# An attention row in another order on TensorE: output product inside the projection, x turned behind the queries and keys, the values' product ahead of the transposes of E

## What is computed

```
h = shift_token(x); q, k, v = split(h @ wqkv, 3)           # 8 heads of 64
q, k = rotary(l2norm(q) * q_scale), rotary(l2norm(k) * k_scale)
sim  = (8 q) k^T, a token sees itself and the tokens before it (the window is all 128)
o    = softmax(sim) @ v
x    = x + o @ wo
```

## Time and profile before

| what | value |
|---|---|
| median of 3 runs | 2650.95 us (2649.64 to 2651.02) |
| profiled execution | 2650.9 us, span 2649.1 us |
| PE busy | 2582.9 us (98%), 25088 matmuls |
| DVE busy | 1916.7 us (72%) |
| ACT busy | 1702.0 us (64%) |
| POOL busy | 1422.8 us (54%) |
| chain that ended last | PE 89%, DVE 4%, issue 3%, ACT 2% |

### The profile page before, as it was taken

One profiled execution on the slowest core, in us unless ns is written; L12 is line 12 of the kernel. 1 busy time (PEld: TensorE's weight loads), 2 busy tenths in 40 slices (PEclk: granted clock), 3 DMA queues, 4 the chain that ended last, 5 costly groups with the idle time before them and its releaser, 6 DMA issues.

```text
span 2649.1 us, 71437 instructions
## 1 busy us (share of the span) xinstructions
PE 2582.9 (98%) x25088; PEld 2221.2 (84%) x25088; DVE 1916.7 (72%) x3779; ACT 1702.0 (64%) x4184; POOL 1422.8 (54%) x1512
## 2 busy tenths in 40 slices
PE   7999999979999999999999999999999999999998
PEld 5888888868888888887888887888888887888887
DVE  7777777668778887786655556788877878666664
ACT  4666666658777777774444446787877777444442
POOL 7888888567777776662100006777777665000000
PEclk9999999989999999999999999999999999999999
DMA  2111111111111111112111111111111111222221
GB/s 47 39 47 37 45 37 37 42 44 39 52 39 50 39 38 42 56 39 79 50 60 56 53 34 49 38 52 39 50 41 36 42 59 34 80 80 73 77 72 48
DMA packets 167250, 130.39 MB, mean 49 GB/s; under 512 B 24870, under 2 KB 165320, under 8 KB 167093
## 3 DMA queue, kind: packets, MB, share of 16 engines
q1 hardware_dynamic: 164789, 119.81, 14.8%
q0 software_dynamic: 2304, 8.47, 1.1%
HBM read 77.47 MB, written 50.33 MB: 48 GB/s over the span
## 4 chain that ended last, share of the span: by engine, by line
PE 89%; DVE 4%; issue 3%; ACT 2%; POOL 1%; DMA 1%; SPq 0%; POOLq 0%; DVEq 0%; ACTq 0%
PE const_banks L1409 6%; PE const_banks L1411 6%; PE const_banks L1410 6%; PE const_banks L1401 6%; PE const_banks L1402 6%; PE const_banks L1403 6%; PE const_banks L1525 5%; PE const_banks L1463 5%; PE const_banks L1499 4%; PE const_banks L1555 3%; PE const_banks L1428 3%; PE const_banks L1429 3%; PE const_banks L1430 3%; PE const_banks L510 3%; PE const_banks L525 3%
## 5 line engine op out<-in xcount | busy, mean ns | idle before, releaser
L1107 ACT ACTIVATE attn_E<-const_banks,attn_nbias,attn_rn 128x128 f32<-128x128 f32 x1024 | 452.9, 462 | 137.8 <-DVE attn_nbias L1314 137.8
L1014 POOL TENSOR_TENSOR attn_qk<-attn_rot_a,attn_rot_b 128x1024 f32<-128x1024 f32 x128 | 303.3, 2370 | 343.3 <-issue 292.5
L1001 POOL TENSOR_TENSOR ffn_rstd<-ffn_var,const_neg_half 128x4 f32<-128x4 f32 x32 | 32.7, 1022 | 645.6 <-DVE ffn_var L1204 645.6
L1409 PE MATMUL const_banks<-weights_w_hi,attn_xT_hi 128*128 128x512 f32 x768 | 315.0, 410 | 3.8 <-ACT attn_sq L1142 3.3
L1411 PE MATMUL const_banks<-weights_w_hi,attn_xT_lo 128*128 128x512 f32 x768 | 303.4, 395 | 0.0
L1410 PE MATMUL const_banks<-weights_w_lo,attn_xT_hi 128*128 128x512 f32 x768 | 303.2, 395 | 0.0
L1225 DVE SCALAR_TENSOR_TENSOR ffn_gated<-const_banks,weights_b_col,ffn_gate 128x512 f32<-128x512 f32 (+1 forms) x192 | 143.7, 748 | 212.1 <-ACT ffn_gate L1085 204.2
L1401 PE MATMUL const_banks<-ffn_xT_hi,ffn_w_hi 128*128 128x512 f32 x704 | 281.7, 400 | 0.7 <-DVE ffn_gated L1225 0.7
L1402 PE MATMUL const_banks<-ffn_xT_lo,ffn_w_hi 128*128 128x512 f32 x704 | 277.9, 395 | 0.0
L1403 PE MATMUL const_banks<-ffn_xT_hi,ffn_w_lo 128*128 128x512 f32 x704 | 277.8, 395 | 0.0
L1085 ACT ACTIVATE ffn_gate<-const_banks,weights_b_col 128x512 f32<-128x512 f32 x160 | 110.0, 688 | 216.2 <-PE const_banks L1403 215.9
(11 more groups left out here) (181 smaller groups left out, 8003.6 us busy)
## 6 DMA issues: line engine op xcount, KB each, us to landing
attn_x_res<-xa SPq DMA_DIRECT2D x128, 128.0 KB, 4.9
xb<-attn_x_new SPq DMA_DIRECT2D x128, 128.0 KB, 1.7
ffn_x_<-xb SPq DMA_DIRECT2D x128, 128.0 KB
h<-ident_h SPq DMA_DIRECT2D x64, 128.0 KB, 1.7
xa<-ident_n SPq DMA_DIRECT2D x64, 128.0 KB, 1.7
attn_x_<-xa SPq DMA_DIRECT2D x128, 64.0 KB
xa<-ffn_x_new SPq DMA_DIRECT2D x16, 512.0 KB, 3.3
ffn_add<-h SPq DMA_DIRECT2D x16, 512.0 KB, 5.0
```

Of the source, the lines that this page charges most:

```text
L1014: pool.tensor_tensor(qk[:, slot].rearrange("p a n -> p (a n)"), rot_a[:].rearrange("p a h d -> p (a h d)"), rot_b[:].rearrange("p a h d -> ...
L1107: last = act.activation(E[:, r, i], ps_s[:, r, i * P:(i + 1) * P], ACT.Exp, bias=nbias[:, r, i:i + 1], scale=rn[:, slot, h:h + 1], accum_o ...
L1409: pe.matmul(out_, xT_hi[:, slot, k], w.w_hi[:, k, cols], start=(k == 0), stop=False)
```

## The change

Within one step of the attention, TensorE's stages come in another order. The output product of row t-5 now stands between queries/keys and values of row t-1. From step 4 on, x of row t is turned behind the transposes of queries and keys, no longer at the start of the step (steps 0 to 3, `EARLY`, keep it there). The values' product of row t-4 stands ahead of the transposes of E of row t-3. ACT's `x_high` moves from ahead of the exponentials to behind `attn_kT`; DVE's `x_low` moves from the start of the step to behind `attn_x_new`, and `attn_x_new` gets one more wait, for `xT_hi` of the same step. No operation is added or removed.

```diff
+        EARLY = (0, 1, 2, 3)
...
-                if on(0) and not (layer and step in (0, 1)):
+                if on(0) and step in EARLY and not (layer and step in (0, 1)):
                     x_high(act, t, u)
...
                     act.activation(kT[:].rearrange("p k n -> p (k n)"), ps_k[:], ACT.Copy).then_inc(s["kT_done"], 1)
+                if on(0) and step not in EARLY:
+                    x_high(act, t, u)
...
-                if on(0) and not (layer and step in (0, 1)):
+                if on(0) and step in EARLY and not (layer and step in (0, 1)):
                     x_low(dve, t, u)
...
                     need(dve, stored[slot], 16 * hf)
+                    need(dve, s["xT_hi"], min_int(t + 1, L + ROWS))
                     dve.tensor_tensor(x_new[:, slot], ps_x[:, D:2 * D], x_res[:, slot], ALU.add).then_inc(s["x_done"], 1)
+                if on(0) and step not in EARLY:
+                    x_low(dve, t, u)
...
-                    queries_keys(pe, b, slot)
-
-                    values(pe, b, slot)
+                    queries_keys(pe, t - 1, (u - 1) % 2)
+                if on(5):
+
+                    b = t - 5
+                    need(pe, s["oT_hi"], b + 1)
+                    need(pe, s["oT_lo"], b + 1)
+                    need(pe, s["xT_lo"], min_int(t, L + ROWS))
+                    need(pe, s["x_done"], b)
...
+                if on(1) and not (layer and step == 1):
+                    values(pe, t - 1, (u - 1) % 2)
                 if step == ROWS + 1:
                     pe.wait_ge(s["et_done"], 2 * (t - 3))
                     group_turn(pe, layer * GROUPS)
...
+                if on(0) and step not in EARLY:
+                    need(pe, s["xT_lo"], t)
+                    need(pe, s["x_done"], t - 5)
+                    turn_row(pe, t, i, u)
+                if on(4):
                     weigh(t, u)
+                if on(2):
+                    need(pe, s["exp_done"], 2 * (t - 2))
...
-                if on(4) and step != ROWS + 2:
-                    weigh(t, u)
```

More of the change, by code:

```diff
@@ L1468, in body @@
                 step = t - L if isinstance(t, int) else None
-                if on(0) and not (layer and step in (0, 1)):
+                if on(0) and step in EARLY and not (layer and step in (0, 1)):
                     need(pe, s["xT_lo"], t)
-                    need(pe, s["x_done"], t - 5)
                     turn_row(pe, t, i, u)
@@ L1478, in body @@
                 elif on(1):
-                    b, slot = t - 1, (u - 1) % 2
                     if step == 1:
                         pe.wait_ge(w.a_low, w.parts)
-                    queries_keys(pe, b, slot)
-                    values(pe, b, slot)
+                    queries_keys(pe, t - 1, (u - 1) % 2)
[5 more added lines that the diff above has]
+                    need(pe, s["x_done"], b)
+                    out_ = ps_x[:, D:2 * D]
+                    for k in range(KI):
+                        pe.matmul(out_, oT_hi[:, k], w.wo_hi[:, k], start=(k == 0), stop=False)
+                        pe.matmul(out_, oT_hi[:, k], w.wo_lo[:, k], start=False, stop=False)
+                        last = pe.matmul(out_, oT_lo[:, k], w.wo_hi[:, k], start=False, stop=(k == KI - 1))
+                    last.then_inc(s["out_ps"], 1)
+                if on(1) and not (layer and step == 1):
+                    values(pe, t - 1, (u - 1) % 2)
                 if step == ROWS + 1:
@@ L1501, in body @@
                         last.then_inc(s[turned], 1)
[L1502 to L1515, removed]
-                    weigh(t, u)
+                if on(0) and step not in EARLY:
[3 more added lines that the diff above has]
+                if on(4):
+                    weigh(t, u)
+                if on(2):
+                    need(pe, s["exp_done"], 2 * (t - 2))
+                    if isinstance(t, int):
+                        pe.wait_ge(s["qT_done"], t - 1)
+                        pe.wait_ge(s["kT_done"], t - 1)
                 if on(3):
```

## The result

The changed kernel takes 2659.91 us (median of 6 runs, 2658.5 to 2662.88) against 2650.74 for the kernel before (6 runs, 2648.45 to 2651.64): ratio 1.0038, 95% interval 1.0025 to 1.0051. It is slower by 9.2 us.

A forecast was written before the change was run, and what follows sets the result against it. The prediction took the chain of DVE and ACT as the bound, 10.04 us a row against PE's 9.86. Terms 3.4 + 1.2 + 0.8 + 1.8 + 1.0 - 0.7 = 7.5 us on 2650.9 gave 2658.4 us, range 2648 to 2668.

The forecast's parts named there:

- the long stretch: Some 105 looped attention rows over both layers: the new order costs 0 to 0.03 us a row, taken as 1.0 us in all.
- PE's row after: PE's own work in one attention row: grows from 9.86 to 10.03 us, just under the 10.04 of DVE and ACT.
- the values' joint: Added fourth change of the array's used part in PE's row, from moving the values' product: one more stop, +0.17 us.
- Step 65: Each layer's step 65: output product waits for `attn_oT_lo`, feed-forward group is turned behind it; +3.4 us layer 1, +1.2 layer 0.
- the clock: Step 65 of either layer: PE's longer idle stretches may lower its clock, 0 to 2.2 us each; 0.4 each taken, 0.8 together.
- the 11.22: Step 65: time from step 64's bias to the first hidden block in the new order at full clock, 11.22 us.
- Written-out rows: Unrolled rows, steps 5 to 7 and 60 to 63 of each layer: PE's longer row costs +1.8 us in all.
- step 4: Step 4 of layer 1: x and some of the product move into PE's 2.05 us of idle time ahead of E, -0.7 us.
- Rival 1: Looped rows: PE was the bound and is freed, the DVE and ACT chain only looked closed; 2641 us, chance 0.10.
- Rival 2: Looped rows: PE becomes the bound, joints cost more than one stop, row 10.10 us (up to 10.20); 2664 us, chance 0.15.
- Rival 3: No change that can be told: the loss at step 65 is half; 2653 us, chance 0.18.
- Rival 4: Every row: the values are late for ACT, 0.1 us a row, +10 us; 2668 us, chance 0.07.

## Why the prediction was right

**The bound and the long stretch.** Right. The row kept 10.04 us, the chain of DVE and ACT was the bound (17.7 us come back when VectorE's loop goes, before, and none after), and PE had 0.18 us of room. The predicted 10.03 of PE's row after is 10.04, and that it came so close is luck, since two errors cancel: the values' joint was priced at 0.17, from the stop of the loads in the earlier trace rows, and measures 0.09; x's turning was taken as free and costs the other 0.09. The written-out rows show too that 10.04 was not what the work of DVE and ACT needs: 0.18 of it came with VectorE's loop. The long stretches cost 1.8 us in the trace against the 1.0 taken. The Trainium skill, "TensorEngine Tiling (Array Packing)", Key Properties, has that a change of the tiling mode drains TensorE. The values' move, which adds such a change, agrees, at 0.09 us; by that rule alone x's move would cost nothing, since it leaves their number as it is, and the trace has 0.09 for it too.

**Step 65.** The mechanism was right in place, order and who waits; the size was off. The prediction had 3.4 in layer 1, 1.2 in layer 0 and 0.8 for the clock, 5.4 in all; the traces have 4.32 and 2.44, 6.8, and putting the order back returns 9.2. The mis-sized term is the clock. Work at the full clock was forecast well: PE began 0.87 us behind the bias where 0.86 was reckoned, and in layer 0, where the clock stayed up until the transposes of E, the exponentials began 4.31 behind it where 4.39 was. Against the 11.22 us from bias to hidden block 12.14 and 12.48 came, 0.9 and 1.3 over, for which 0.4 each was taken. In the five other kernels with the product first at step 65 the stretch took 13.1 to 14.3 us. And the 10.04 us of layer 0 before was itself an execution with the clock down: with the group first, layer 0 took 7.34 to 8.85 us in six other kernels and 10.04 in one, so 1.2 was the price against a row with the clock down.

**Written-out rows and step 4.** Biases 0 to 7 and 57 to 62 hold both terms, 1.8 and -0.7, and took 0.9 us more where 1.1 was forecast. How it splits can't be read from one pair: PE's idle time at step 4 of layer 1 did shrink, from 2.05 to 0.76 us, but biases 0 to 7 of that layer took 70.78 us after 70.44, and 69.2 to 71.2 in the other kernels with VectorE's and TensorE's loops. The stretch between the layers gave 0.7 back, which was not foreseen; it takes 413.7 to 416.2 us in all the traces, so it need not be the change's.

**Sum and rivals.** 2658.4 predicted, 2659.91 measured. In the traces 6.8 of the 8.9 us lie at step 65, where 5.4 were forecast, and 2.1 elsewhere, as forecast, though these include the 0.7 that the stretch between the layers gave back. Rival 1 (PE was the bound) is ruled out: PE's room before is measured. What the prediction said against it, that PE waits for DVE and ACT and not they for it, overlooked a row of the same view: DVE waits for PE's queries and keys ahead of `attn_rot_a` in all 51 rows, 19.9 us. It cost nothing because DVE then waited for ACT's exponentials anyway, 0.36 us at 810.42. Rival 2 was close: PE did become level with the chain, at 10.04 rather than 10.10. Rival 3 (half the loss at step 65) is ruled out by the 9 us that come back. Rival 4 cost no time but came near: the copy of the values did come to wait for PE, 10.9 us in 34 of 51 rows, and the slack ahead of the squares took this up. Their wait fell from 0.8 to 0.14 us a row, nearer its end than the 0.3 us of room that was reckoned.

## What to carry to other kernels

- Two resources nearly level (10.04 and 9.86 us a row) hide a cost, they don't remove it: the 0.18 us a row that this change spent is worth some 18 us (0.18 x 102 rows) once the other bound is lifted. Lift the bound first and judge an order then.
- When an order is changed in a loop, look at the steps where the loop runs out: nearly the whole loss came from two steps, one in each layer, at which the first instruction left in the queue was one that waits.
- A price for idle time on TensorE includes the clock behind it: here about 1 to 3 us over the 11.22 worked out for the full clock, in the six kernels with the product first at step 65, in which TensorE stood idle for some 3 us once or twice.

## What the runs showed of the hardware

- In the order of before, VectorE's looped rows took 0.18 us a row more than the same instructions written out in layer 0 and 0.15 in layer 1, TensorE's a further 0.04 (9.86 to 9.82) and 0.06, ScalarE's none that shows. In the order of after, where PE needs 10.04 itself, VectorE's loop costs nothing that shows. Of VectorE's, a wait of 0.2 us between two of its own instructions went; whether the register in the wait or the jump makes it was not separated.
- From the start of a pair of 128x128 transposes to the start of what follows it takes 0.19 us ahead of a 512-column product and 0.31 ahead of products of 64 columns of weights. Here this was as large a cost as one more change of the used part of the array, 0.09 us a row each.
